# A Macaron block with attention on one core: the six part products in another order, and the subtraction of the maxima between the two halves of the scores

## The reference

```python
x = x + 0.5 * ffn(layernorm(x))            # x: 16 x 256 x 128, 8 experts
x = x + attn(layernorm(x))
x = x + 0.5 * ffn(layernorm(x))
# attn: 16 heads of width 8, batch 16, length 256
scores = einsum('bhqd,bhkd->bhqk', Q, K) / SCALE
scores = scores + einsum('bhqd,qkd->bhqk', Q, pek[idx]) / SCALE   # idx = clip(k - q) + 128
attn   = softmax(where(causal, scores, -inf))
out    = einsum('bhqk,bhkd->bhqd', attn, V) + einsum('bhqk,qkd->bhqd', attn, pev[idx])
return out.transpose(...).reshape(b, s, D) @ Wo.T
```

## Time and profile before

| | us |
|---|---|
| median of 3 runs | 971.23 |
| lowest and highest run | 966.93 and 976.51 |
| the profiled execution | 967.66 |
| its span (first to last instruction) | 965.9 |

### The profile page before, as it was taken

One profiled execution on the slowest core, in us unless ns is written; L12 is line 12 of the kernel. 1 busy time (PEld: TensorE's weight loads), 2 busy tenths in 40 slices (PEclk: granted clock), 3 DMA queues, 4 the chain that ended last, 5 costly groups with the idle time before them and its releaser, 6 DMA issues.

```text
span 965.9 us, 29195 instructions
## 1 busy us (share of the span) xinstructions
PE 636.5 (66%) x12366; PEld 516.7 (53%) x12366; DVE 504.7 (52%) x1712; ACT 297.2 (31%) x473; POOL 235.6 (24%) x227
## 2 busy tenths in 40 slices
PE   4512998700733789888898879899972811689640
PEld 3501556500422678777787768788862800357430
DVE  7977222123721567565666557667766777512120
ACT  2390454300522232323232313232332264063210
POOL 2000738884533000000000000014110000346864
PEclk9999999955885599999898979999985555599985
DMA  4272213325355332323222323234342506112322
GB/s 122 59 218 80 53 17 43 34 24 142 132 160 173 92 62 70 59 69 60 69 44 74 52 70 56 65 72 97 75 110 46 175 1 178 24 35 31 45 25 22
DMA packets 99163, 73.27 MB, mean 76 GB/s; under 512 B 26569, under 2 KB 92258, under 8 KB 98914
## 3 DMA queue, kind: packets, MB, share of 16 engines
q1 hardware_dynamic: 85858, 57.01, 23.4%
q0 software_dynamic: 13184, 14.43, 9.2%
HBM read 44.34 MB, written 27.01 MB: 74 GB/s over the span
## 4 chain that ended last, share of the span: by engine, by line
PE 38%; DVE 15%; POOL 14%; issue 11%; ACT 9%; SPq 6%; DMA 5%; DVEq 0%; ACTq 0%; POOLq 0%
PE banks L1002 10%; ACT arena L778 8%; PE banks L1005 7%; POOL x_mid L554 5%; PE banks L1025 5%; POOL out_dram L554 5%; SPq L469 3%; DVE arena L1119 3%; PE banks L1066 2%; PE banks L849 2%; POOL arena L543 2%; PE banks L929 2%; PE banks L913 1%; DMA out_dram<-arena 1%; SPq L440 1%
## 5 line engine op out<-in xcount | busy, mean ns | idle before, releaser
L778 ACT ACTIVATE arena<-banks 128x1024 f32<-128x1024 f32 x96 | 98.3, 1024 | 263.4 <-PE banks L1025 263.4
L1002 PE MATMUL banks<-arena 128*128 128x32 bf16 x3072 | 126.8, 194 | 42.8 <-issue 16.1
L1002 PEld LDWEIGHTS banks<-arena 128*128 128x128 bf16 x3072 | 112.4, 101 | 68.1 <-ACT arena L778 38.7
L1366 DVE TRANSPOSE_TENSOR_REDUCE arena<-banks 128x32 f32<-128x1024 f32 x96 | 120.0, 1250 | 18.1 <-PE banks L1005 13.8
L1005 PE MATMUL banks<-arena 128*128 128x32 bf16 x3072 | 108.6, 178 | 8.6 <-issue 8.6
L1005 PEld LDWEIGHTS banks<-arena 128*128 128x128 bf16 x3072 | 93.6, 97 | 11.3 <-issue 11.3
L543 POOL DMA_INDIRECT arena<-table,arena x64 | 61.5, 961 | 126.2 <-DVE arena L1276 107.7
L607 POOL COPY arena<-arena 128x576 f32 (+1 forms) x8 | 5.3, 668 | 329.6 <-PE banks L1056 329.6
L1382 DVE TENSOR_REDUCE arena<-banks 32x8 f32<-32x64 f32 (+1 forms) x96 | 20.1, 209 | 107.9 <-PE banks L1017 107.8
L710 ACT ACTIVATE arena<-banks,arena 128x512 f32<-128x512 f32 x64 | 44.0, 687 | 85.2 <-PE banks L929 85.2
L1025 PE MATMUL banks<-arena 128*128 128x64 bf16 x1536 | 64.4, 198 | 0.7 <-issue 0.7
(11 more groups left out here) (182 smaller groups left out, 1021.4 us busy)
## 6 DMA issues: line engine op xcount, KB each, us to landing
query_parts<-arena SPq DMA_DIRECT2D x8, 768.0 KB, 6.4
arena<-query_parts SPq DMA_DIRECT2D x16, 384.0 KB
table<-arena SPq DMA_DIRECT2D x2, 2176.0 KB, 9.4
arena<-in_L_ffn_fc2s_dram SPq DMA_DIRECT2D x4, 1024.0 KB, 10.8
arena<-query_parts SPq DMA_DIRECT2D x16, 256.0 KB
key_parts<-arena SPq DMA_DIRECT2D x8, 384.0 KB, 7.0
arena<-key_parts SPq DMA_DIRECT2D x8, 384.0 KB
head_outputs<-arena SPq DMA_DIRECT2D x128, 18.0 KB
```

The lines of the kernel that those rows point to most:

```text
L778: nc.scalar.activation(dst, psum[:, 2 * r:2 * r + 2, :].rearrange("p u (h n) -> p u h n", h=H), ACT.Exp, scale=HD ** -0.5).then_inc(s_prob, 1)
L1002: pe.matmul(sc[:, :, 2 * a:2 * a + 2], rel_k[:, y:y + P], q_st[:, r, :, q0 + 2 * a:q0 + 2 * a + 2], start=(a == 0), stop=False, skip_group ...
L1366: step(v.tensor_reduce(mp, psum[:, 2 * (s % 3):2 * (s % 3) + 2, :].rearrange("p u (h n) -> p (u h) n", n=32), AX.X, ALU.max, apply_transpo ...
```

## The change

Two edits. The six part products come in another order: run 0 to 2 is now (query, key) parts (0,2), (1,1), (2,0), run 3 to 4 is (0,1), (1,0), run 5 is (0,0). The key parts are stored in reverse order, so that both a query load and a key load of n terms read n neighbouring, different parts. Number and bytes of the loads stay. And `subtract_maxima(s - 2)` moves from behind the scores of slot s to between their two halves, right behind `turn_maxima(s - 1)`.

```diff
-        Q_PART = (0, 0, 0, 1, 1, 2)
-        K_PART = (0, 1, 2, 0, 1, 0)
+        Q_PART = (0, 1, 2, 0, 1, 0)
+        K_PART = (2, 1, 0, 1, 0, 0)
...
-                    q = qs[c, Q_PART[a], 0:HD, :, bass.ds(pr * PT, PT)]
-                    q = q.unsqueeze(0).to_broadcast([b - a, HD, H, PT])
-                    k = ks[0:b - a, :, :, bass.ds(pr * PT, PT)].rearrange("w d h n -> (w d) h n")
+                    q = qs[c, 0:b - a, :, :, bass.ds(pr * PT, PT)].rearrange("w d h n -> (w d) h n")
+                    k = ks[3 - (b - a):3, :, :, bass.ds(pr * PT, PT)].rearrange("w d h n -> (w d) h n")
...
             if i % 2:
-                return k_part[:, i // 2 % 2, w, :]
+                return k_part[:, i // 2 % 2, 2 - w, :]
...
-                def scores(s, pr, r, turn):
+                def scores(s, pr, r, turn, between):
...
                         if u == 0 and turn:
                             turn_maxima(s - 1, pr)
+                        if u == 0 and between:
+                            subtract_maxima(s - 2, pr)
...
-                        scores(s, pr, r, turn=s >= 1 or not first)
-                        if s >= 2 or not first:
-                            subtract_maxima(s - 2, pr)
+                        scores(s, pr, r, turn=s >= 1 or not first, between=s >= 2 or not first)
```

## The result

The changed kernel takes **998.6 us** (median of 4 runs, 993.1 to 1002.0) against 969.1 for the kernel before in the same comparison: ratio 1.029, interval 1.021 to 1.038. It is slower; 931 was forecast. The profiled execution took 1001.96 us, its span is 1000.2.

What follows compares the result with a forecast made beforehand. Bounds: before the pairs, stores and query loads on three DMA engines; in the pairs, the scores, subtraction, exponential chain. Savings 25 + 2 + 9 + 4 = 40 us from the median 971.2 gave 931; range 912 to 950, own range 918 to 944.

Steps and rivals of the forecast that it cites:

- the gaps: PE's stops at the pair's start with nothing named, nine coming to 26 us; no change taken, ends -12 and +10.
- part 1: New order of the parts, loads spread over more engines: -25 us before the pairs, -2 us in the pairs.
- the slower rival: In the pairs, loads on all sixteen engines add gaps of PE: 983 us, deciding from 5.7 us more per pair; chance 0.03.
- Before the pairs: Stage making and storing parts: PE starts at 287 instead of 311.9, -25 us, ends -28 and -10.
- ACT's waits for stores: Sign in the stage before the pairs: ACT's first-part waits fall from 34 us to under 10.
- Slot 9: In the pairs, PE's stand at slot 9 behind a store queued after the loads goes: -2 us.
- The moved subtraction: Slots of the pairs go from 3.64 to 3.48 us: -9 us over seven pairs, ends 0 and -17; pair 0 counted separately.
- 4 in pair 0: Pair 0, where DVE's loop sets the pace after the move: -4 us, ends -2 and -7.
- DVE's delay: In a pair's four slots with `reduce_relative`, slack falls to 0.15 us; +0.2 each, +0.35 for an adjoining second: +0.95 a pair.
- my sign that DVE would release L1017 in slots 2, 3, 5 and 7: In the pairs' slots 2, 3, 5 and 7, DVE's L1368 would be the releaser of L1017; no size given.

Runs made afterwards that it cites:

- the spaced kernel: The changed kernel, but SP issues the next pair's loads one a slot, with the store that slot 9 needs ahead of them; 926.9 us, ratio 0.955.

## Why the prediction was wrong

**The step that failed** is the one on the gaps: "They lie where loads are in flight. I take no change; ends -12 (half go) and +10." Measured: from 27.8 to 92.6 us, +65. Behind it stands a figure of part 1: "At the key load's 195 GB/s the 2.36 MB of a pair take 12 us." They take 25. I had taken a rate from one window of 1 us, with two loads in flight (while key loads run, windows of 2 us show 131 and 135 GB/s in the kernel before), and asked only how many DMA engines a load has, not what it writes. With 25 us instead of 12, at a share of 0.6 to 1.1, the sentence against the slower rival ("the new bursts are less than half as long") is wrong too. The old form moved 70 GB/s on three engines and the new one 60 to 145 on most of them: little faster, and much more in the way. That the slowdown needs loads in flight, many engines, many loads at once and slow writes is shown by the runs without later loads, with nine rows a part, with one or three at a time, and with more lanes. That PE waits for its instructions is shown by the packets of q8: every gap of the changed kernel ends within 1.9 us behind one. The Trainium skill, page "Runtime: NRT & Kernel Launch", section "Instruction fetch mechanics", has instructions fetched in 16 KiB blocks over DMA; the page of the profile agrees with 102 packets and 1.67 MB on a queue called instruction, 16 KB each. Why the packets come late is argued: no row tells which DMA engine carries one, so that they stand behind the loads on the same engines is inferred from the runs above.

**The slower rival** was the right one, down to its place and the point from which it decides (5.7 us a pair; measured 65 / 7 = 9). It had a chance of 0.03 and should have had much more, since nothing in the trace bounded the gaps from above: that three engines were busy during the old gaps said nothing about sixteen.

**Before the pairs**: forecast -25, measured -16.9 (PE starts at 295.06, not 287), inside its ends. The mechanism is right, but loads and stores together did not reach the 342 GB/s that I gave them: windows with both show 255 GB/s from 282 to 285 us and 246 from 288.5 to 290.5, at shares of 1.02 and 0.82. The narrow writes of the loads are the likely reason; no run separates it. ACT's waits for stores fell to 15.8 us, not under 10.

**Slot 9**: -2 forecast, and the stand is gone. That faster slots run into the stores behind narrow loads is shown by the run with nine rows (three stands, 8.6 us in all) and by the subtraction alone (4.39 us), though not in every pair.

**The moved subtraction**: 13 forecast (9 in the pairs, 4 in pair 0), 8 to 14 measured. The slot went to 3.47, against 3.48 forecast. DVE's delay, which I had put at 0.95 us a pair, did not come: in pairs 1 to 6 PE waits for DVE nowhere. In the spaced kernel the waits from 295 to 668 us are

```profile
PEld banks L1027 <- DVE arena L1376: 5.6, 9, 1.1
```

and none of these nine, and none of the changed kernel's nine, lies between 335 and 640 us; they are in pairs 0 and 7. So the slack of 0.15 us was enough, and my sign that DVE would release L1017 in slots 2, 3, 5 and 7 failed. Slots are still not all equal. In pair 4 of the spaced kernel three go 3.46, 3.86 and 3.62:

```profile
480.78 0.54 PEld L1010 LDWEIGHTS banks<-arena 128*128 128x128 bf16 x16 [0.20 <-issue]
...
484.24 0.54 PEld L1010 LDWEIGHTS banks<-arena 128*128 128x128 bf16 x16 [0.20 <-issue]
...
486.81 0.24 PEld L1013 LDWEIGHTS banks<-arena 128*128 128x128 bf16 x7 [0.32 <-issue]
...
488.10 0.54 PEld L1010 LDWEIGHTS banks<-arena 128*128 128x128 bf16 x16 [0.20 <-issue]
...
490.56 0.96 PEld L1076 LDWEIGHTS banks<-arena 128*32 128x32 f32 x32
...
491.72 0.36 PEld L1010 LDWEIGHTS banks<-arena 128*128 128x128 bf16 x10 [0.20 <-issue]
```

The 3.86 holds 0.32 us of idle without a releaser in the middle of its scores, which ends 1.4 us behind a packet of q8 as the gaps do; the 3.62 holds a chunk of 0.96 us in place of 0.81. In pair 0, where DVE does set the pace, full slots take 3.22 to 3.27 us in the spaced kernel, against 3.3 forecast at the high clock and 4.19 before.

**The sum by measured terms.** From pair 0's first scores to the last turn of the maxima the kernel before takes 392.4 us (311.9 to 704.3), the changed one 444.4 (295.0 to 739.4): +52. Gaps +65, slot 9 -2, subtraction -8 to -14 make +49 to +55. With -17 before the pairs and -1 behind them that is the +34 of the spans. The lower clock (0.86 against 0.95) comes with the gaps; what it costs by itself was not separated.

The kernel with one load a slot came to 926.9, near the 931 of the forecast. Its terms are like the forecast's in kind: -17, -2, -8 to -14, and gaps unchanged. They make -27 to -33 of the 44 us that it gained, so that the totals agree so well is in part luck; the higher clock (0.97 against 0.95) may be some of the rest. What the forecast described was that kernel, not this one.

## What to carry to other kernels

Before spreading a transfer over more DMA engines, find what limits it: here the side it writes was narrow, so more engines only meant that more of them were held for nearly the same time (25 us against 28), and the kernel's own instructions came late. Look at share and GB/s together over the whole burst, never at one window of it. Where an engine stands in the middle of equal instructions and no one is named, look in the DMA view for packets of the instruction queue. When a background transfer must be wide, give it out in pieces at the pace of the work; check what else is behind it in the same queue and move the urgent stores ahead.

## What the hardware showed that I had not expected

Nine loads queued at once stopped PE for up to 10.95 us in the middle of a row of matmuls, though none of the waits of the program is open, and each such stop ended 1.3 to 1.9 us behind a 16 KB packet of instructions. A load into 24 lanes ran at 145 GB/s on most engines and at 70 on three; the loads into 8 lanes ran at 57 GB/s in the kernel before (384.9 to 388 us, share 0.57) and at 60 in the changed one (share 0.57); and the same bytes into 32 to 96 lanes at 196 to 249. A source written with the parts as a dimension of their own was issued at the pace of the merged one (nine loads in 10 us), and only a gap in memory brought back the slow pace (28 us).
